# A two-layer frequency and spatial mixing block: three groups of stacked spectra held, strips split and pixels turned a step sooner, spectra copied out of PSUM by DVE

## What is computed

```python
xm = einsum('bchw,oc->bohw', x, W_in)                  # 32 -> 3 * 85 channels
x_spatial, x_freq, x_gate = split(xm, 3, axis=1)
out_spatial = depthwise_conv_3x3(x_spatial, W_dw)      # SAME padding
xf = rfft2(x_freq in patches of 8 x 8) * fft_weight    # one weight a channel and frequency
out_freq = irfft2(xf)
x_fused = gelu(x_gate) * (out_spatial + out_freq)
return einsum('bchw,oc->bohw', x_fused, W_out)         # 85 -> 32 channels
```

## Time and profile before

| what | us |
|---|---|
| three runs: median (lowest to highest) | 876.5 (872.7 to 879.3) |
| the profiled execution, its own time | 879.0 |
| its span, first to last instruction | 877.2 |
| busy PE / PEld | 790.4 / 672.1 |
| busy DVE / ACT / POOL | 559.1 / 573.0 / 643.5 |
| mean granted TensorE clock (1 is 2.4 GHz) | 0.96 |

### The profile page before, as it was taken

How to read it: one execution, slowest core, us unless ns; L and a number is a source line. 1 busy time by engine, 2 the same in 40 slices (tenths; PEclk the granted TensorE clock), 3 DMA queues, 4 the chain that set the end, 5 groups by cost and what they waited for, 6 DMA issues and landing times.

```text
span 877.2 us, 32629 instructions
## 1 busy us (share of the span) xinstructions
PE 790.4 (90%) x12840; PEld 672.1 (77%) x12840; DVE 559.1 (64%) x956; ACT 573.0 (65%) x1087; POOL 643.5 (73%) x1101
## 2 busy tenths in 40 slices
PE   3586989889999799988999979999899999899997
PEld 2375878768778678877887868887788888788886
DVE  7585767568767676666766646666666566466543
ACT  2564757566677577766777757766767677577764
POOL 2675867698678888777777958777777778678781
PEclk9698999899999999999999989999999999899999
DMA  8469557955566756656565546767656776656651
GB/s 292 121 165 248 120 115 183 234 130 128 125 167 157 172 125 148 145 137 165 151 160 151 139 130 163 190 175 187 161 143 173 182 182 175 180 148 169 185 152 49
DMA packets 91297, 140.80 MB, mean 161 GB/s; under 512 B 28530, under 2 KB 31658, under 8 KB 90762
## 3 DMA queue, kind: packets, MB, share of 16 engines
q1 hardware_dynamic: 64182, 110.89, 49.1%
q0 software_dynamic: 26336, 27.40, 12.8%
q10 hardware_dynamic: 628, 0.44, 0.2%
HBM read 10.98 MB, written 8.56 MB: 22 GB/s over the span
## 4 chain that ended last, share of the span: by engine, by line
PE 47%; POOL 19%; DMA 15%; issue 8%; ACT 6%; DVE 3%; ACTq 1%; POOLq 0%; SPq 0%; DVEq 0%
PE ps_s L474 18%; DMA xs<-xf 14%; POOL xs L357 9%; POOL yl L772 8%; PE ps_ft L529 7%; PE ps_z L567 4%; PE ps_s L576 3%; PE ps_s L579 3%; PE ps_s L577 3%; PE ps_g L480 3%; PE ps_o L540 3%; ACT yh L703 2%; ACT turned_results L691 1%; PE ps_xt L442 1%; ACT xt L654 1%
## 5 line engine op out<-in xcount | busy, mean ns | idle before, releaser
L474 PE MATMUL ps_s<-cw,stack 128*128 128x85 f16 (+1 forms) x7168 | 456.0, 206 | 1.7 <-DVE f L1024 1.7
L474 PEld LDWEIGHTS ps_s<-cw,stack 128*128 128x128 f16 (+1 forms) x7168 | 377.1, 100 | 27.7 <-DVE f L1024 2.3
L357 POOL DMA_DIRECT2D xs<-xf x754 | 377.2, 505 | 11.9 <-issue 9.5
L772 POOL TENSOR_TENSOR yl<-y,yh 128x340 f16<-128x340 f32 x256 | 231.1, 903 | 183.6 <-ACT yh L703 181.6
L703 ACT ACTIVATE yh<-y 128x340 f16<-128x340 f32 x256 | 124.6, 487 | 205.3 <-PE ps_s L579 192.3
L1056 DVE TENSOR_TENSOR y<-ps_z,weff 128x340 f32<-128x340 f32 x256 | 130.1, 508 | 141.4 <-PE ps_z L567 136.8
L955 DVE TENSOR_TENSOR parts<-xn,parts 128x1024 f16<-128x1024 f32 (+2 forms) x99 | 124.7, 1261 | 93.9 <-ACT parts L630 93.7
L1024 DVE TENSOR_TENSOR f<-ps_s,g 128x340 f32<-128x340 f32 x256 | 130.1, 508 | 67.2 <-PE ps_s L579 66.9
L529 PE MATMUL ps_ft<-squares_sb,f 128*85 128x128 f32 x1024 | 167.5, 287 | 0.8 <-ACT turned_results L691 0.8
L691 ACT ACTIVATE turned_results<-ps_ft 85x512 f32<-85x512 f32 x256 | 149.4, 584 | 28.5 <-PE ps_ft L529 28.2
L696 ACT ACTIVATE g<-ps_g,gsc 128x340 f32<-128x340 f32 x256 | 137.4, 537 | 38.6 <-PE ps_g L480 38.1
(11 more groups left out here) (107 smaller groups left out, 728.1 us busy)
## 6 DMA issues: line engine op xcount, KB each, us to landing
stack<-parts SPq DMA_DIRECT2D x496, 130.0 KB, 3.4
xs<-xf POOLq DMA_DIRECT2D x754, 32.0 KB, 2.3
out_y<-yo SPq DMA_DIRECT2D x16, 512.0 KB, 2.9
stack<-parts SPq DMA_DIRECT2D x124, 65.0 KB, 2.5
stack<-parts SPq DMA_DIRECT2D x124, 64.5 KB, 2.4
stack<-parts SPq DMA_DIRECT2D x124, 64.0 KB, 2.3
x<-in_x SPq DMA_DIRECT2D x3, 2048.0 KB, 10.4
x<-in_x SPq DMA_DIRECT2D x4, 512.0 KB, 5.9
```

The lines of the kernel that those rows point to most:

```text
L357: eng.dma_start(xs[C * k:C * k + C, h % 2, q, :], xf[C * q:C * q + C, h % 2, SPECTRA[k], :]).then_inc(loaded, 16)
L474: mm(ps_s[i % 2][:, HID * q:HID * (q + 1)], pixels(kind, i, q, dy, rows), w[0:rows, m, :], start=(q == 0 and m == 0), stop=False)
L772: nc.gpsimd.tensor_tensor(yl[:, k, :], y32[:, k, :], yh[:, k, :], ALU.subtract).then_inc(s_yl, 1)
```

## The change

- xs has three slots (HELD) for two. Loads of group h are issued at 4h-7 (six), 4h-6 and 4h-5 (three each).
- The split of a strip (from strip 3 on) and the turning of its pixels stand one step sooner: pair p is turned at 2p-13 and transformed at 2p-12. Turns are now in odd steps.
- From group 2 on the high half of a spectrum is written by DVE out of PSUM (`spectrum_out`), right ahead of the low half, at 4h-8 behind f. ACT keeps this for groups 0 and 1.
- f is written over g in place. The residual of a group stands at the end of DVE's step i % 4 = 2 instead of in the step behind it.
- At the beginning pairs 0 and 1 are turned at once into two banks, and only they are transformed ahead of the loop; pairs 2 and 3 follow in steps -2 and -1. The first stack and spectrum loads are shared out otherwise over SP, POOL and ACT.
- A gathered statistic is read three steps after its gather instead of four, statistics of images 2 and 3 stand in other steps, the weights of layer 1 are made some 13 steps sooner, ACT's split waits for the loads of the strip before last (`strip_loaded`), out_edge has one slot, and `ones` lies in a spare part of another tile.

```diff
...
-DRAIN = 4
-WARM = (6, 4, 8, 4, 6)
+DRAIN = 3
+WARM = (2, 20)
...
 PAIR, GROUP = 2, 4
+HELD = 3
...
-FIRST_LOADS = [[(PAIRS_HI[0::2], PAIRS_LO[0::2], THIRDS[0::3]), (PAIRS_HI[1::2], PAIRS_LO[1::2], THIRDS[1::3]),
-                ([], [], THIRDS[2::3])],
+FIRST_LOADS = [[(PAIRS_HI[0:2] + PAIRS_HI[4:6] + PAIRS_HI[8:9], PAIRS_LO[0::2], THIRDS[0:4]),
+                (PAIRS_HI[2:4] + PAIRS_HI[6:8] + PAIRS_HI[9:12], PAIRS_LO[1::2], THIRDS[4:9]), ([], [], THIRDS[9:12])],
...
+FIRST_SPECTRA = [[(0, 0), (0, 1), (0, 2), (2, 0), (2, 1)], [(1, 0), (1, 1), (1, 2), (1, 3), (0, 3), (2, 2), (2, 3)]]
...
-READ, AGGREGATE = 1, 5
-SUMMING = {1: range(8), 2: (17, 21, 25, 26, 29, 33, 34, 37), 3: (49, 53, 57, 61, 65, 66, 69, 70)}
+READ, AGGREGATE = 1, 4
+SUMMING = {1: range(8), 2: (17, 19, 21, 25, 27, 29, 33, 35), 3: (49, 51, 53, 57, 59, 61, 65, 67)}
...
-        xs = sb("xs", [3 * C, 2, Q, GROUP * 128], F16)
+        xs = sb("xs", [3 * C, HELD, Q, GROUP * 128], F16)
...
-        f = sb("f", [128, 2, GC])
+        xts = [xt, yh[:, :, :].rearrange("p k o -> p (k o)")[:, 0:PAIR * 2 * 128].rearrange(
+            "p (a b n) -> p a b n", a=PAIR, b=2)]
...
-            strip, at = i // TPS + 2, i % TPS
+            strip, at = (2, i) if i < TPS - 1 else ((i + 1) // TPS + 2, (i + 1) % TPS)
...
-            if piece == 0:
-                for q in range(Q):
-                    load_spectrum(eng, 0, q, s_xs_first[0][by], (by,))
             eng.wait_ge(s_xl, before + ORDER.index(1) + 1)
             for load in lo:
                 load_pair(eng, 0, load, loaded[0], a, z)
+            if piece == 0 and by < 2:
+                for k, q in FIRST_SPECTRA[by]:
+                    load_row(eng, 0, q, k, s_xs_first[0][by])
...
         def turns_at(p):
-            return PAIR * p - 12 if p >= 8 else p - 4
+            return PAIR * p - 13 if p >= 9 else p - 4
+        def transforms_at(p):
+            return turns_at(p) + (1 if p >= 4 else 0)
         def leaves_at(h):
-            return turns_at(2 * h + 1) + 2
+            return {1: 0, 2: 3, 3: 5}[h] if h < 4 else GROUP * h - 8
         def loads_at(h, q):
-            return 4 * h - 6 + q if h > 2 else (3, 3, 4, 4)[q]
-        turning = {turns_at(p): p for p in range(4, PAIRS)}
-        transforming = {turns_at(p) + 1: p for p in range(4, PAIRS)}
-        leaving = {leaves_at(h): h for h in range(2, GROUPS_OF_TILES)}
-        def load_spectrum(eng, h, q, loaded, rows=range(3)):
-            need(eng, s_z, GROUP * (h - 1))
-            for k in rows:
-                eng.wait_ge((s_xfh, s_xfl)[SPECTRA[k]], h + 1)
-                eng.dma_start(xs[C * k:C * k + C, h % 2, q, :],
-                              xf[C * q:C * q + C, h % 2, SPECTRA[k], :]).then_inc(loaded, 16)
+            return {2: (3, 3, 4, 4), 3: (6, 6, 7, 8)}[h][q] if h < 4 else GROUP * h - 7 + (0, 0, 1, 2)[q]
+        turning = {turns_at(p): p for p in range(2, PAIRS)}
+        transforming = {transforms_at(p): p for p in range(2, PAIRS)}
+        leaving = {leaves_at(h): h for h in range(1, GROUPS_OF_TILES)}
...
+        def load_row(eng, h, q, k, loaded):
+            need(eng, s_z, GROUP * (h - HELD + 1))
+            eng.wait_ge((s_xfh, s_xfl)[SPECTRA[k]], h + 1)
+            eng.dma_start(xs[C * k:C * k + C, h % HELD, q, :],
+                          xf[C * q:C * q + C, h % 2, SPECTRA[k], :]).then_inc(loaded, 16)
+        def load_spectrum(eng, h, q, loaded):
+            for k in range(3):
+                load_row(eng, h, q, k, loaded)
...
-                need(pe, s_xt, p)
+                need(pe, s_xt, p if p != 1 else 0)
+                bank = ps_s[1] if p == 1 else ps_xt
...
                 if p % 2 == 0:
-                    need(pe, s_xfh, p // 2)
                     need(pe, s_xfl, p // 2)
+                turned_pixels = xts[1] if p == 1 else xt
...
-            for p in range(4):
-                turn(p)
-                warm(WARM[p])
-                transform(p)
-            warm(WARM[4])
+            turn(0)
+            turn(1)
+            warm(WARM[0])
+            transform(0)
+            transform(1)
+            warm(WARM[1])
...
                     need(pe, s_ft, i - 2)
                     for q in range(Q):
                         t = nc.tensor.transpose(ps_ft[0:HID, q * 128:(q + 1) * 128],
-                                                f[:, k, HID * q:HID * (q + 1)], id32)
+                                                g[:, k, HID * q:HID * (q + 1)], id32)
...
-                if i in turning:
+                if i in turning and i >= 0:
                     turn(turning[i])
                 if live(i, 0):
                     gate(i, range(Q // 2, Q)).then_inc(s_gate, 1)
                     conv(i, 2)
-                if i == -1:
-                    conv_begins(0)
-                    conv(0, 0)
-                    conv(0, 1)
...
                     z.then_inc(s_z, 1)
+                if i == -1:
+                    conv_begins(0)
+                    conv(0, 0)
+                    conv(0, 1)
+                if i in turning and i < 0:
+                    turn(turning[i])
...
                 if dx == ORDER[0]:
-                    need(act, s_s, (strip - 2) * TPS + 1)
-                    if strip == 2:
-                        for by, loads in enumerate(FIRST_LOADS[1]):
-                            for kind in range(2):
-                                act.wait_ge(s_first[1][by][kind], count(loads, kind))
+                    if strip >= 2:
+                        strip_loaded(act, strip - 2)
...
             def turned_over(p):
                 act.wait_ge(s_xt_made, p + 1)
-                need(act, s_dft, p)
-                nc.scalar.activation(xt[:, :, :, :].rearrange("p a b n -> p (a b n)"), ps_xt[:, :],
-                                     ACT.Copy).then_inc(s_xt, 1)
+                need(act, s_dft, p if p != 1 else 0)
+                nc.scalar.activation((xts[1] if p == 1 else xt[:, :, :, :]).rearrange("p a b n -> p (a b n)"),
+                                     (ps_s[1] if p == 1 else ps_xt)[:, :], ACT.Copy).then_inc(s_xt, 1)
...
             turned_over(0)
+            turned_over(1)
             hi_of_projection(0)
+            hi_of_spectrum(0)
             hi(0, ORDER[2], slice(*PIECES[0]))
-            turned_over(1)
+            act.wait_ge(s_xn, 4)
+            hi(0, ORDER[0], slice(*PIECES[1]))
             hi_of_taps(0)
-            hi_of_spectrum(0)
...
-            act.wait_ge(s_xn, 4)
-            hi(0, ORDER[0], slice(*PIECES[1]))
+            for n in (6, 11, 12, 13, 10):
...
             load_piece(act, 0, 2)
-            turned_over(2)
-            for n in (6, 10, 11, 12, 13):
-                placing(0, n)
-            turned_over(3)
...
-            hi_of_spectrum(1)
...
-                if i in leaving:
-                    hi_of_spectrum(leaving[i])
+                if i == 0:
+                    hi_of_spectrum(1)
...
                 if live(i, 0):
                     need(act, s_gate, i + 1)
-                    need(act, s_f, i - 1)
+                    need(act, s_ftp, i - 1)
                     nc.scalar.activation(g[:, i % 2, :], ps_g[:, 0:GC], ACT.Gelu,
                                          scale=gsc[layer(i)][:, 0:1]).then_inc(s_gelu, 1)
-                if i in turning:
+                if i in turning and i != -1:
                     turned_over(turning[i])
...
+                if i == -1:
+                    turned_over(turning[i])
...
-                if i == 54:
+                if i == 38:
                     hi_of_projection(1)
-                if i == 55:
+                if i == 46:
                     hi_of_taps(1)
...
-                nc.gpsimd.tensor_copy(out_edge[:, side, :], x[:, b, :, (BW - 1) * side]).then_inc(s_out_edge, 1)
+                nc.gpsimd.tensor_copy(out_edge[:, :], x[:, b, :, (BW - 1) * side]).then_inc(s_out_edge, 1)
...
-                if i in (-1, 0):
-                    load_spectrum(pool, 1, i + 3, s_xs_first[1][1])
-                for h in range((i + 3) // GROUP, (i + 6) // GROUP + 1):
+                if i == 0:
+                    for q in (2, 3):
+                        load_spectrum(pool, 1, q, s_xs_first[1][1])
+                for h in range((i + 4) // GROUP, (i + 7) // GROUP + 1):
                     for q in range(Q):
                         if 2 <= h < GROUPS_OF_TILES and loads_at(h, q) == i:
-                            load_spectrum(pool, h, q, s_xs[h % 2])
+                            load_spectrum(pool, h, q, s_xs[h % HELD])
...
+            def spectrum_out(h):
+                dve.wait_ge(s_dft, 2 * h + 2)
+                if h < 4:
+                    for by in range(2):
+                        dve.wait_ge(s_xs_first[h - 2][by], 16 * (len(FIRST_SPECTRA[by]) if h == 2 else 2 * 3))
+                else:
+                    dve.wait_ge(s_xs[(h - 2) % HELD], 16 * 3 * Q * ((h - 4) // HELD + 1))
```

(46 more changed lines are left out.)

60 lines of the change are left out of this document (33 added, 27 removed).

## The result

| | before | after |
|---|---|---|
| median of the runs, us | 877.65 (4 runs, 872.7 to 879.3) | 864.39 (4 runs, 862.0 to 865.5) |
| ratio to before, 95% interval | | 0.9855 (0.9808 to 0.9901) |
| span of the profiled execution | 877.2 | 862.9 |
| granted clock | 0.96 | 0.99 |

A forecast was written before the change was run, and what follows sets the result against it. PE, busy 90% of the span, was taken to set the time, interrupted by late xs loads. 879.0 - 72.0 - 5.4 + 50 - 5 = 846.6 us, put at 844 on the scale of the median; range 822 to 866.

The forecast's parts named there:

- The mechanism: Waits for xs nearly gone after tile 12; instead about 60 transform waits for DVE's xf, alternating near 0.4 and 1.0 us.
- the unknown instruction: DVE's new high-half copy, 512 columns out of PSUM, in no trace: taken as 0.68 us, with 0.38 for the range.
- the first term, 72.0 us: Tiles 12 to 243: three slots win back the whole loss, 747.7 us against 58 groups at 11.65.
- given back there: Transform waits for DVE's spectra, 0.44 us at a strip's start, 1.01 mid-strip: 42 us, plus 4 and 4, together 50.
- tiles 4 to 11: Three slots gain only one step at the 6.0 us wait in step 10: 5.4 us of the 12.4 lost won.
- up to tile 3: The beginning, with only pairs 0 and 1 ahead of the first spectral matmul: 5 us gained, bounds 0 and 8.
- Costs of nothing: Changes put at no cost: f over g, moved turns, strip_loaded, statistics three steps after gather, earlier layer 1 weights, one out_edge.
- The 0.5 us put on 8 strips: Layer 0: residual, statistics and edge column pass about 0.5 us to the next step's f in 8 strips: 4 us.
- The transfers stay late: Rival: half of the 72 us loss by late loads stays, 36 us more, 880 us, no difference; chance 0.06.
- DVE late at every spectrum: Rival: groups at a strip's start wait 1.01 us instead of 0.44, 17 us more, 861 us; chance 0.18.
- The chain does not hold PE: Rival: DVE's f, high and low halves do not delay the transform; 50 us not given back, about 798; chance 0.09.
- the slower rival: DVE's chain in step 4h-8: mean wait of 1.42 us a group returns to 879, 1.7 gives 896; chance 0.05.

The follow-up runs named there:

- e1: Kernel after, with DVE writing both halves of a spectrum one step sooner (4h-9, from group 4 on): 823.62 us.
- e3: Kernel after, with DVE reading each spectrum once more out of PSUM ahead of its high half (62 added instructions): 906.12 us.
- e5: Kernel after, with ACT writing the high half of every spectrum again and DVE only the low half: 859.8 us.
- e9: Kernel after, with splits and turns back in the steps of the kernel before; DVE's copy, three slots and new beginning stay: 816.96 us.
- e4: Kernel before, with three slots for the stacked spectra, their earlier loads and f written over g alone: 819.07 us, ratio 0.944.
- e10: The kernel of e9, with gathered statistics read four steps after the gather instead of three: 812.28 us.
- e2: Kernel after, with SP issuing the 2 MB load of image 2 behind the stack loads of strip 2 instead of strip 1: 857.88 us.
- e7: Kernel after, with spectra written at 4h-9, image 2 loaded behind strip 2, and layer 1 weights made in the steps of the kernel before: 823.62 us.

## Why the prediction was partly right and where it failed

**The mechanism was right.** The waits for xs went, the transform's waits for DVE's xf came, in number (60), pattern (a short and a long one in turn) and sum (50.9 us in the list). e1, e3, e5 and e9 show from four sides that the cause is the step which the chain shares with the transform. The cost of the unknown instruction was right as well: 0.679 us in the mean of 62 (group of the new high half: busy time, mean ns of one, idle time ahead of it).

```profile
L1003 DVE TENSOR_SCALAR xf<-ps_x 128x512 f16<-128x512 f32 x62 | 42.1, 679 | 0.0
```

The low bound of 0.38 us was never near: the shortest of the 62 took 0.672 us. Of the 0.66 to 0.68 us that the prediction gives this instruction, 0.68 is what L971 took; the 0.66 stands on no run, and measured were 0.672 to 0.681.

**The step that failed is the first term, 72.0 us.** It took every microsecond above 11.65 a group in tiles 12 to 243 for the work of the late transfers, theirs and the clock's, and so for something that three slots take away. They took away 55 to 56: 17.0 us stay in e4 (353.0 and 339.7 us for the two stretches against twice 337.9) and 15.8 in e10 (351.5 and 340.0). Nor was the floor at fault: 46 of the 58 groups of e10 took 11.65 us within 0.1. What stays stands in a few groups, 12.5 of the 15.8 us in six of them (tiles 12, 40, 72, 76, 104 and 136), and in each of the six PE waits for POOL's yl, 8.9 us together. This yl is the first one behind the issues of a gather, which POOL makes in steps 9, 37, 41, 69, 73, 101 and 133; only the one of step 41 is followed by no such wait. (The six waits for yl in e4, 6.1 us, stand in tiles 40, 44, 72, 76, 104 and 136, behind the gathers of steps 37 to 133.) POOL and then PE in e10, around tile 40 (timeline):

```profile
162.65 2.21 POOL L754 DMA_DIRECT2D gathered<-sums  x4
164.85 0.53 POOL L775 DMA_DIRECT2D edge<-out_edge  x1
165.37 1.00 POOL L376 DMA_DIRECT2D xs<-xf  x2
168.35 0.50 POOL L376 DMA_DIRECT2D xs<-xf  x1 [1.98 <-issue]
168.86 0.84 POOL L793 TENSOR_TENSOR yl<-y,yh 128x340 f16<-128x340 f32 x1
...
169.75 0.32 PE L606 MATMUL ps_s<-yl,inv 128*128 128x340 f16 x1 [2.52 <-POOL yl L793]
```

In the kernel before, four of these six groups (40, 72, 104, 136) were among its seven longest, 15.7 to 18.3 us, each with a long wait for xs; the sum charged all of that to the transfers, and when the transfers came in time, a second wait stood in the same groups. That the gathers delay yl is read from the order on POOL; no run moved or left out a gather. The prediction counted twelve issues and four yl a group for POOL and found that it had room (9.07 us busy in 11.65, read in tiles 60 to 63, where no gather stands); the gathers and edges that POOL issues between them were not in that count.

Term by term, from the ends of tiles in the two profiled executions, with e10 as the kernel without the shift:

| term | forecast | measured |
|---|---|---|
| late transfers gone, tiles 12 to 243 | -72.0 | -56.2 (before 747.7, e10 691.5) |
| given back there | +50 | +50.5 (after 742.0) |
| tiles 4 to 11 | -5.4 | -4.6 |
| up to tile 3 | -5 | -4.0 |
| sum | -32.4 | -14.3 |

With e9, which differs from the kernel after by the shift alone, the first two lines are -52.4 and +46.7.

The second line was right partly by luck. Counted from the floor the kernel after lies 66.3 us above it in these groups, not 50, and 15.8 of that e10 has too. The transform's waits alone are 49.4 us of idle time there, which lengthened the 58 groups by about 58.7 (0.16 more each); 50 were forecast. The reaction of PE to DVE's semaphore was put at 0.05 us and is 0.15, which is 6 us over 58 groups. "Costs of nothing" had at least one entry that was not nothing: the gathered statistic came late, with PE behind it, 5.3 us in tiles 12 to 15 (18.1 against 12.8 in e2; named there as a risk, and not put in the sum). The weights of layer 1 may be a second: one of their pieces, 0.94 us, stands ahead of f in the group of tile 48, which waited 2.30, but e7 lost more with the pieces in their old steps. The 0.5 us put on 8 strips for residual, statistics and edge column was not evenly there: strips of layer 0 without an edge column waited 0.38 as in layer 1 (tiles 24, 32, 56, 64, 96), those behind one of 0.40 us 0.42 to 0.52 (tiles 16, 72, 104), those behind longer ones 1.48 to 2.30 (48, 80, 112).

**The rivals.** "The transfers stay late" is out in the kernel after: no wait for xs beyond tile 11. "DVE late at every spectrum" is the nearest in number (861) and wrong in mechanism: groups at a strip's start in layer 1 wait 0.38, not 1.0. "The chain does not hold PE" is out by e9. In layer 0 single groups came near the price of the slower rival (2.30 us in tile 48's), the mean did not.

**The stack loads** held PE once in the kernel after, for 0.9 us in tile 8, and hardly more without the waits: 2.6 and 2.3 us in tile 8 of e1 and e9, 0.45 in layer 1 of e4. All three run layer 1 within 2 us of the floor.

## What to carry to other kernels

Before a wait is charged with all the time above the best stretch, ask group by group what else stands in the same steps: when the first wait goes, the engine that comes second holds the same groups, here POOL with its gathers ahead of yl. The best stretch can be right as a floor, and yet not every group reaches it. When a schedule is moved by a step, look at every pair of producer and consumer that the move brings into one step: here a copy, its remainder and the transform that reuses their bank, which before had a step between them and the transform. Making one part alone is worth a run: three slots without the shift gave 49 to 58 us, all parts together 13.

## What the runs showed of the hardware

The waits of the transform cost more than their idle time in the list: in layer 1 of the kernel after 0.38 and 0.95 us of idle time lengthened the groups by 0.54 and 1.11, 0.16 each time. The matmuls in the timeline overlap where nothing holds PE (L579 runs until 808.28, and L474 behind it began at 808.11), by 0.17 us there, about what a wait cost above its idle time.

PE went on 0.15 us after the end of the low half that it waited for, in the median of the transform's 60 waits in the kernel after.

PE's pace went with the granted clock. In the kernel before the 340 columns of L577, from its start to that of L579, took 0.143 us where the granted clock was 1.00 (median of 243 tiles) and 0.285 where it was 0.50 (of 10): 2.4 and 1.2 columns a ns, the pace that the 2.4 and 1.2 GHz of the prediction stand for. The stretch 496.0 to 514.3 of the earlier trace rows holds both clocks, 1.00 until 506.0 and 0.50 from 508.0 to 513.0.

The clock did not follow the length of a single wait. In all these traces every group behind tile 3 whose longest wait of PE was 1.69 us or less kept a mean clock of 1.00. From 1.7 to 2.6 us it went either way: 1.73 us gave 0.89 in the group of tile 48 of the kernel before, 2.30 gave 1.00 in that of the kernel after and 2.35 again 0.89 in e2; in e3, waits of 2.27 us left 1.00 in four groups (tiles 36, 52, 60, 68) and gave 0.89 in one (28). Five groups of e3 in layer 0 (tiles 8, 20, 28, 48, 112) so lost 1.7 to 1.8 us more than their waits, about 1.6 of it beyond the 0.16. Groups with a wait of 2.7 us or more all showed 0.91 or less.

A small transfer was late behind a large one: the first sums<-st landed after 7.3 to 9.8 us in the traces with the 2 MB load of image 2 issued ahead of it, and after 3.5 to 4.7 where that load stood a strip later.
